# A decoder layer on one core: q and k normalised, turned and scaled beside the projection, and two groups of scores ahead of a turn

## What is computed

```python
qkv = jnp.clip(jnp.einsum('bsd,ed->bse', hidden_states, Wqkv), -8.0, 8.0)
q, k, v = jnp.split(qkv, [D_MODEL, 2 * D_MODEL], axis=-1)
q = _layer_norm(q, q_ln_w, q_ln_b)
k = _layer_norm(k, k_ln_w, k_ln_b)
# 32 heads of 32
scores = jnp.einsum('bqhd,bkhd->bhqk', q, k) * scale + slopes * rel   # causal
out = jnp.einsum('bhqk,bkhd->bqhd', softmax(scores), v).reshape(B, S, D_MODEL)
...
x = x + _L0_attn_ref(_layernorm(x), ...)
x = x + _L0_xattn_ref(_layernorm(x), ctx_4096, ctx_4096, ...)   # softmax of q over the head, of k over the positions
x = x + _L0_ffn_ref(_layernorm(x), ...)
```

## Time and profile before

| What | Value |
|---|---|
| Median of 3 runs | 3303.28 us (3303.07 to 3303.88) |
| Span of the profiled execution | 3299.9 us |
| What lies around the span, median less span | 3.4 us |
| TensorE busy | 3128.8 us, 95% |
| Weight loads busy | 2393.9 us, 73% |
| VectorE busy | 1773.3 us, 54% |
| ScalarE busy | 1045.8 us, 32% |
| GpSimd busy | 507.1 us, 15% |
| Mean granted TensorE clock | 0.977 of full |
| Moved by the transfers | 66 GB/s on average |

### The profile page before, as it was taken

The page is one execution under the profiler, slowest core; times in us unless marked ns, Lnnn a source line. Parts: engine busy times, 40 slices in busy tenths (PEclk is TensorE's granted clock), DMA queues, the critical chain, the costliest instruction groups (busy, mean ns, idle before and its releaser), DMA issues. The chain is left out here.

```text
span 3299.9 us, 41826 instructions
## 1 busy us (share of the span) xinstructions
PE 3128.8 (95%) x15136; PEld 2393.9 (73%) x15136; DVE 1773.3 (54%) x2927; ACT 1045.8 (32%) x2356; POOL 507.1 (15%) x525
## 2 busy tenths in 40 slices
PE   7999997799999999999996799999999899999998
PEld 6888886566666666666663688888887788888887
DVE  5311112466666666666663655555555655555555
ACT  2100000566665566666651211111111211111111
POOL 2100000233333333333332100000000100000000
PEclk9999999899999999999996899999999999999999
DMA  4222223111111111111110432222122521231222
GB/s 144 93 73 75 73 70 116 41 39 38 43 46 51 38 38 39 50 38 51 38 33 31 129 82 55 76 65 75 54 82 76 153 64 54 81 81 54 62 74 78
DMA packets 83350, 218.73 MB, mean 66 GB/s; under 512 B 11984, under 2 KB 18256, under 8 KB 81232
## 3 DMA queue, kind: packets, MB, share of 16 engines
q1 hardware_dynamic: 83280, 217.78, 21.8%
HBM read 175.79 MB, written 41.94 MB: 66 GB/s over the span
## 5 line engine op out<-in xcount | busy, mean ns | idle before, releaser
L312 PE MATMUL ff_ps<-h_xT_hi,w_hi 128*128 128x512 f32 x1376 | 538.2, 391 | 13.2 <-DVE h_xT_lo L96 13.2
L312 PE MATMUL ff_ps<-h_xT_lo,w_hi 128*128 128x512 f32 x1376 | 537.1, 390 | 0.0
L312 PE MATMUL ff_ps<-h_xT_hi,w_lo 128*128 128x512 f32 x1376 | 537.0, 390 | 0.0
L1042 ACT ACTIVATE w_hi<-words 128x1024 fp32r<-128x1024 f32 x134 | 142.5, 1063 | 697.3 <-DVE words L1087 697.3
L1127 DVE TENSOR_TENSOR acc<-ff_po,acc 128x512 f32<-128x512 f32 x352 | 243.0, 692 | 210.6 <-PE ff_po L312 209.9
L312 PE MATMUL qkv_acc<-w_hi,xT_hi 128*128 128x512 f32 x768 | 300.9, 392 | 9.2 <-DVE w_lo L255 9.2
L312 PEld LDWEIGHTS ff_ps<-h_xT_hi,w_hi 128*128 128x128 f32 x1376 | 259.5, 189 | 68.3 <-issue 8.8
L312 PE MATMUL qkv_acc<-w_hi,xT_lo 128*128 128x512 f32 x768 | 299.4, 390 | 0.0
L312 PE MATMUL qkv_acc<-w_lo,xT_hi 128*128 128x512 f32 x768 | 299.3, 390 | 0.0
L312 PEld LDWEIGHTS ff_ps<-h_xT_hi,w_lo 128*128 128x128 f32 x1376 | 259.4, 189 | 54.1
L312 PEld LDWEIGHTS ff_ps<-h_xT_lo,w_hi 128*128 128x128 f32 x1376 | 259.6, 189 | 53.8
(11 more groups left out here) (156 smaller groups left out, 5305.9 us busy)
## 6 DMA issues: line engine op xcount, KB each, us to landing
words<-in_w SPq DMA_DIRECT2D x90, 512.0 KB, 3.5
qkv<-qkv_out SPq DMA_DIRECT2D x96, 256.0 KB, 2.0
words<-in_w SPq DMA_DIRECT2D x176, 128.0 KB, 4.0
sc<-in_s SPq DMA_DIRECT2D x88, 256.0 KB, 4.3
qk_in<-qkv SPq DMA_DIRECT2D x16, 1024.0 KB, 4.9
w_stage<-in_w_attn SPq DMA_DIRECT2D x56, 256.0 KB, 3.0
qkv_rows<-in_x SPq DMA_DIRECT2D x16, 512.0 KB, 3.8
ctx_in<-in_context SPq DMA_DIRECT2D x16, 512.0 KB, 3.7
```

The lines of the kernel that those rows point to most:

```text
L312: last = nc.tensor.matmul(out, left, right, start=n == 0, stop=n == len(pairs) - 1)
L1042: nc.scalar.activation(dst, src, ACT.Copy).then_inc(s["split_hi"], 1)
```

## The change

**The projection** now works in two halves of eight tiles. Each half goes through all six chunks, so there are twelve rounds of eight tiles, and the weights are read twice. A round loads the eight pieces of the next one, one with every tile. The first chunk is loaded at once into the room of `head_left`, in four loads. Behind the second chunk of q, and of k, a tile's 1024 columns lie whole in SBUF (`head_left`, `head_right`). VectorE adds their statistics, GpSimd normalises (`normalise_heads`), TensorE turns them one tile later (`turn_heads`), ScalarE scales them (`scale_heads`), and SyncE stores them into `qh` and `kh` two tiles later. In round 5 the x tiles of the second half are loaded, normalised, turned and split.

**The attention** loads q as it is and k straight into the blocks of `kD` (`load_heads`). `transpose_qk`, `norm_qk_affine`, `qk_statistics`, `normalise_qk` and `key_blocks` go. A turn's first two groups of scores, its first tile of keys with the exponentials and transposes, the transposes of group 0's probabilities and the context's transposes are now done in the tail of the turn ahead of it (`second_lead`, `lead_scalar`), or, for turn 0, ahead of the loop. The twelve steps follow with everything two steps earlier (j for t - 2). The reciprocal norms are spread by eight transposes of a column that is read 128 times, in place of the diagonal matrix. The memset of `kD` stands first in the attention's setup, and SyncE waits for it. Outside these phases only unused semaphores and a size of scratch memory for transfers change.

The core of the diff:

```diff
+    TILES = NB // 2
+    ROUNDS = 2 * QKV_CHUNKS
+    xT_hi = sb("xT_hi", [P, TILES, KT, P], F32R, ph)
+    xT_lo = sb("xT_lo", [P, TILES, KT, P], F32R, ph)
...
+            def load(ci, r):
+                sp.wait_ge(s["w_lo_done"], ci * KT + r - 1)
+                chunk = ci % QKV_CHUNKS if ci < ROUNDS else QKV_CHUNKS
+                sp.dma_start(stage[:, r % 2, :], w_attn[chunk, :, r, :]).then_inc(w_in[r % 2], 16)
+
+            def load_rows(n):
+                if n >= 2:
+                    sp.wait_ge(ln.transposed, n + 1)
+                sp.dma_start(rows[:, n % 2, :], x[n, :, :]).then_inc(x_in[n % 2], 16)
+
+            def store_heads(m):
+                half, kind, t = m // (2 * TILES), m // TILES % 2, m % TILES
+                sp.wait_ge(s["h_out"], m + 1)
+                sp.dma_start((qh, kh)[kind][half * TILES + t, :, :],
+                             flat(heads[:, m % 2, :, :])).then_inc(h_stored[m % 2], 16)
...
+            for ci in range(ROUNDS):
+                half, chunk = half_and_chunk(ci)
+                for t in range(TILES):
+                    load(ci + 1, t)
+                    if ci == 0 and t + 3 < TILES:
                         load_rows(t + 3)
-                    if t % 2 == 0:
-                        load(c + 1, t // 2)
-                    sp.wait_ge(clipped, c * NB + t + 1 + BANKS)
-                    sp.dma_start(qkv[t, :, bass.ds(c * N, N)], res[:, :]).then_inc(stored, 16)
-
-            chunks(sp, chunk)
-            sp.wait_ge(stored, 16 * (QKV_CHUNKS * NB + 1))
+                    if ci == 4 and t < 2:
+                        load_rows(TILES + t)
+                    if (m := follows(ci, t, 2)) is not None:
+                        store_heads(m)
+                    if chunk >= 4:
+                        n = values_before(ci, t)
+                        sp.wait_ge(s["clipped"], ci * TILES + t + 1)
+                        sp.dma_start(v[half * TILES + t, :, (chunk - 4) * N:(chunk - 3) * N],
+                                     res[:, n % 2, :]).then_inc(v_stored[n % 2], 16)
+                    if ci == 5 and t + 2 < TILES:
+                        load_rows(TILES + t + 2)
...
+            def normalise_heads(m):
+                t, p = m % TILES, m % 2
+                pool.wait_ge(s["h_mom"], m + 1)
+                nc.gpsimd.tensor_tensor(h_mom[:, p, 4:5], h_mom[:, p, 3:4], half_neg[:, :], ALU.pow).then_inc(
+                    s["h_rstd"], 1)
+                pool.wait_ge(s["h_rstd"], m + 1)
+                for part in (left[:, t, :], right[:, p, :]):
+                    last = nc.gpsimd.tensor_scalar(part, part, h_mom[:, p, 2:3], h_mom[:, p, 4:5], ALU.add, ALU.mult)
+                last.then_inc(s["h_normed"], 1)
...
+            def scale_heads(m):
+                kind = m // TILES % 2
+                if m == 0:
+                    act.wait_ge(s["affine_in"], 4 * 16)
+                act.wait_ge(s["h_turned"], m + 1)
+                if m >= 2:
+                    act.wait_ge(h_stored[m % 2], m // 2 * 16)
+                for k in range(KT):
+                    last = nc.scalar.activation(heads[:, m % 2, k, :], room[m % 2][:, k, :], ACT.Identity,
+                                                scale=affine[:, 2 * kind, k:k + 1],
+                                                bias=affine[:, 2 * kind + 1, k:k + 1])
+                last.then_inc(s["h_out"], 1)
...
+                if chunk < 4:
+                    dve.wait_ge(s["clipped"], at + 1)
+                    first = chunk % 2 * 6
+                    nc.vector.bn_stats(h_stats[:, t, first:first + 6], dst).then_inc(s["h_stats"], 1)
...
+            def part(ci, t):
+                hi, lo, at = w_hi[ci % 2], w_lo[ci % 2], ci * TILES + t
+                for k in range(KT):
+                    if ci == 0 and t == 0:
+                        pe.wait_ge(s["w_lo_done"], k + 1)
+                    for n, (a, w) in enumerate(((xT_hi, hi), (xT_hi, lo), (xT_lo, hi))):
+                        last = nc.tensor.matmul(acc[:, at % 4, :], a[:, t, k, :], w[:, k, :],
+                                                start=k == 0 and n == 0, stop=k == KT - 1 and n == 2)
+                last.then_inc(s["mm_done"], 1)
...
+            def turn_heads(m):
+                pe.wait_ge(s["h_normed"], m + 1)
+                if m >= 2:
+                    pe.wait_ge(s["h_out"], m - 1)
+                for k in range(KT):
+                    part_of = (left[:, m % TILES, :], right[:, m % 2, :])[k // 4]
+                    last = nc.tensor.transpose(room[m % 2][:, k, :], part_of[:, k % 4 * P:(k % 4 + 1) * P], ident[:, :])
+                last.then_inc(s["h_turned"], 1)
...
+                    part(ci, t)
+                    if (m := follows(ci, t, 1)) is not None:
+                        turn_heads(m)
+                    if ci == 5:
+                        if t == 0:
+                            pe.wait_ge(s["h_out"], 2 * TILES)
+                        ln.transpose(pe, TILES + t, t % 2, room[t % 2])
...
+    def load_heads(sp, b):
+        sp.dma_start(hT[:, :, :], qh[b, :, :].rearrange("p (a d) -> p a d", a=KT)).then_inc(s["q_loaded"], 16)
+        for j in range(HG):
+            at = slice(j * HD, (j + 1) * HD)
+            sp.dma_start(kD[at, :, j, :], kh[b, at, :].rearrange("p (a d) -> p a d", a=KT)).then_inc(s["kd_loaded"], 16)
+
+    def scores(pe, b, t):
+        nc.tensor.matmul(bank_s[:, :], hT[:, t, :], flat(kD[:, t, :, :]), start=True, stop=True).then_inc(
+            s["s_done"], 1)
...
         if ahead:
-            pe.wait_ge(s["p_out"], (b + 1) * G)
+            pe.wait_ge(s["q_loaded"], (b + 2) * 16)
+            pe.wait_ge(s["kd_loaded"], (b + 2) * HG * 16)
             if cross:
                 pe.wait_ge(s["y_out"], b)
             else:
-                pe.wait_ge(s["s_biased"], (b + 1) * G)
-            transpose_qk(pe, b + 1)
+                pe.wait_ge(s["m_out"], (b + 1) * XT)
+            scores(pe, b + 1, 0)
...
+            keys(pe, b + 1, 0)
         if cross:
-            if ahead:
-                pe.wait_ge(s["a_out"], 2 * b + 4)
-            pe.wait_ge(s["n_diag"], c + 1)
-            for e, bank in enumerate(norm_banks):
-                last = nc.tensor.matmul(bank, ones[:, :], flat(diag[:, 4 * e:4 * e + 4, :]), start=True, stop=True)
+            pe.wait_ge(s["n_pow"], c + 1)
+            pe.wait_ge(s["y_out"], c + 1)
+            for k in range(KT):
+                last = nc.tensor.transpose(norm_banks[k // 4][:, k % 4, :],
+                                           n_sq[:, 1, k:k + 1].to_broadcast([P, P]), ident[:, :])
             last.then_inc(s["r_done"], 1)
+        if ahead:
+            second_lead(pe, b + 1)
...
+    def second_lead(pe, b):
+        pe.wait_ge(s["s_biased"], b * G + 1)
+        scores(pe, b, 1)
+        turn_probabilities(pe, b, 0)
+        turn_keys(pe, b, 0)
+        pe.wait_ge(s["kt_out"], b * XT + 1)
+        transpose_context(pe, b)
...
         if ahead:
-            norm_qk_affine(act, b + 1)
-            context_out(act, b + 1)
+            lead_scalar(act, b + 1)
+
+    def lead_scalar(act, b):
+        exponentials(act, b, 0)
+        key_exponentials(act, b, 0)
+        exponentials(act, b, 1)
+        probabilities_out(act, b, 0)
+        keys_out(act, b, 0)
+        context_out(act, b)
...
+            key_maxima(dve, b + 1, 0)
...
+            bias_scores(dve, b + 1, 1)
+            maxima(dve, b + 1, 1)
+            reciprocals(dve, b + 1, 1)
```

More of the change, by code:

```diff
@@ L235, in _ @@
+            for r in range(KT // 2):
                 high(0, r, w_hi[0])
-            ln.high(act, 0, 0, turn[0])
-            for r in range(PIECES // 2, PIECES):
+            ln.high(act, 0, 0, room[0])
+            for r in range(KT // 2, KT):
                 high(0, r, w_hi[0])
-            def chunk(c, parity, first):
-                if not first:
-                    act.wait_ge(mm_done, c * NB)
-                for t in range(NB):
-                    if first and t + 1 < NB:
-                        ln.high(act, t + 1, t + 1, turn[(t + 1) % 2])
-                    if t % 2 == 0:
-                        high(c + 1, t // 2, w_hi[1 - parity])
@@ L249, in _ @@
-            chunks(act, chunk)
+            for ci in range(ROUNDS):
+                if ci:
+                    act.wait_ge(s["mm_done"], ci * TILES)
+                for t in range(TILES):
+                    if ci == 0 and t + 1 < TILES:
+                        ln.high(act, t + 1, t + 1, room[(t + 1) % 2])
+                    high(ci + 1, t, w_hi[1 - ci % 2])
+                    if (m := follows(ci, t, 1)) is not None:
+                        scale_heads(m)
+                    if ci == 5:
+                        ln.high(act, TILES + t, t, room[t % 2])
@@ L265, in _ @@
             statistics(1)
-            for r in range(1, PIECES // 2):
+            for r in range(1, KT // 2):
                 low(0, r, w_hi[0], w_lo[0])
-            ln.low(dve, 0, 0, turn[0])
```

(39 more changed lines are left out.)

592 lines of the change are left out of this document (288 added, 304 removed).

## The result

The changed kernel takes 3328.61 us (median of 4 runs: 3326.89, 3327.0, 3330.23 and 3357.04), before 3303.18. The slowest of the four had a granted clock of 0.917 where the others had 0.97; with it the ratio of the means is 1.0097 (95% interval 1.0078 to 1.0116), without it 1.0075 and the median 3327.0. The kernel is slower by 25.4 us, by 23.8 without that run; forecast were 3321 and slower.

The account below looks back on a forecast made before the run. TensorE, close to full in all three stages, was taken as the bound. Terms -9.5 + 29.1 + 6.6 + 0.5 - 4.5 - 5.0 + 3.8 - 3.2 = +17.8 on 3303.3 gave 3321 us; range 3296 to 3343, its own 3310 to 3332.

Parts of the forecast that it names:

- Prologue: Start of the projection: first weights land in four loads, so products start at 14.6, not 24.07; -9.5 us.
- Head transposes: Projection: 32 head tiles at 0.91 us each on TensorE, with no wait ahead of them; +29.1 us.
- contention that I kept as a rival: Projection: GpSimd and VectorE contend, so a head tile's chain outgrows its 6.35; +5 us, 3326, double at most; chance 0.07.
- Half boundary: Round 5 into round 6: VectorE falls behind on x tiles, the eighth weight piece is late; 5.1 plus 1.5 clock, +6.6 us.
- Weight supply: Value rounds of the projection: load loop of 5.4 against 5.44 just holds, last piece 0.25 late at two rounds' starts; +0.5 us.
- products in the value rounds wait: Sign in the projection's value rounds by which the prediction called itself wrong; no size given.
- rival 4: Value rounds: weight pieces land in 3.8, not 3.0, so the loop is 6.2; +22 us, 3343; chance 0.10.
- Transition: Projection's end to turn 0: 45.0 becomes 40.5, output weights landing 23.6 behind the products; -4.5 us, bounds -7 and 0.
- Tails: Turns 1 to 14: waits of 0.65 and 3.3, -9.8 us, and clock falls in every turn, +13.6; together +3.8.
- tail of turn 0: End of attention turn 0: 25.17 becomes 18.7 with waits of 1.4 and 2.5, plus 1.5 for the clock; -5.0 us.
- Last turn: End of the attention: diagonal product goes, two matmuls of 1.9 each become eight transposes of some 2.0 in all; -3.2 us.
- rival that the lead hides its waits: Attention tails: all 3.95 per turn and the clock falls go, decided at ScalarE's exponentials of group 1; 3240; chance 0.08.

Follow-up runs that it names:

- doubled run: On the changed kernel, the eight transposes of a head tile in the projection run twice over, same result: 3355.8 us, 27.2 more.
- run with the weights first: On the changed kernel, SyncE issues the output weights' four loads ahead of q and key blocks, and they are split ahead of other setup: 3324.36 us, 4.2 less.
- run with the keys first: On the changed kernel, ScalarE copies the turned keys out ahead of the exponentials of group 1: 3275.4 us, 53.2 less.
- filled run: On the changed kernel, three more passes of the tail's eight key transposes, same place and values, run where TensorE would stand: 3309.8 us, 18.8 less.

## Why the prediction was right, point by point

**Prologue, right.** 24.07 to 14.78 is 9.3; forecast 9.5.

**Head transposes, right, both the price and that nothing hides them.** 32 x 0.91 fill the stage's sum below, and the doubled run adds 0.86 for each tile. The contention that I kept as a rival didn't come: the six rows of `w_lo` that take 0.80 to 1.43 all lie in round 0, beside GpSimd's normalising of x as in the earlier trace rows. In the head rounds VectorE's subtraction never runs beside GpSimd's halves. At 4 of the 32 head tiles it ends ahead of them, at the other 28 it starts 0.15 to 0.22 behind their end, held until then by ScalarE's `w_hi`:

```profile
72.89 0.68 DVE L321 TENSOR_TENSOR w_lo<-w_stage,w_hi 128x512 fp32r<-128x512 f32 x1
...
80.90 0.69 DVE L321 TENSOR_TENSOR w_lo<-w_stage,w_hi 128x512 fp32r<-128x512 f32 x1 [2.48 <-ACT w_hi L284]
```
```profile
74.08 0.77 POOL L263 TENSOR_SCALAR head_left<-head_left,head_mom 128x512 f32<-128x512 f32 x1
...
79.91 0.77 POOL L263 TENSOR_SCALAR head_right<-head_right,head_mom 128x512 f32<-128x512 f32 x1
```

What the Trainium skill says of shared SBUF interfaces (GPSIMD Engine Reference, section Specifications) fits the rows of 1.43. In the head rounds the two miss each other by 0.2; the prediction had no reason for that, so this part of it is luck.

**Half boundary, the mechanism right, the sum right by luck.** Ahead of the first product of round 6 and in it 4.1 + 2.5 = 6.6 were lost (a tile step of 10.46 in place of 6.36, then 7.91 in place of 5.44), as forecast. VectorE does fall behind as I had it, by 0.7 to 1.1 a tile. It starts the statistics of the last x tiles 7.12 and 7.44 apart (the last of these three rows is at 301.92), where TensorE's tile takes 6.35:

```profile
287.36 0.69 DVE L63 BATCH_NORM_STATS2 ln_stats<-qkv_rows 128x6 f32<-128x512 f32 x1 [3.12 <-DMA qkv_rows<-in_x]
...
294.48 0.69 DVE L63 BATCH_NORM_STATS2 ln_stats<-qkv_rows 128x6 f32<-128x512 f32 x1 [3.01 <-DMA qkv_rows<-in_x]
```

But TensorE had more room than I gave it: it waits 0.70 and 2.97, where I had 0.7, 1.1 and 3.3, so 3.7 for 5.1. The fall of the clock behind them, 2.5 of it in the first product of round 6, makes most of the other 2.9, for which I had 1.5. Two misses of opposite sign make the 6.6.

**Weight supply, mis-sized.** Forecast +0.5, measured 1.2 and 1.3 at the starts of rounds 5 and 11. The median landing of all pieces is 3.3, not 3.0; in round 4 ScalarE starts on most pieces 3.1 to 3.3 behind their issue, on the first 3.8. So the loop takes 5.6 against 5.44, and the eighth piece is late. By its own words the prediction was wrong "if products in the value rounds wait": they do, twice for 1.0, far from the 22 of rival 4. -9.3 + 29.1 + 6.6 + 2.5 = +28.9, against a measured +29.0.

**Transition, the term that failed.** Forecast -4.5, measured -0.3. I had all four loads of the output weights landed 23.6 behind the products. The first was split at 24.5, the last at 28.3, since they land 1.25 apart behind the loads of q, of the key blocks and of the rest. VectorE's lead starts behind the last subtraction, at 620.0, 30.5 behind, where I had 25.9. The run with the weights first shows that cause.

**Tails, the waits right within 0.2, the turn and the clock mis-sized.** 0.65 and 3.3 were forecast, 0.49 and 3.25 came, and by the released engine and its order: the run with the keys first takes 2.14 off. What was off is the fall's price. I took 1.51 a turn from the kernel before. It was 1.6 in every second turn and 2.6 in the others. In all of them the context's transposes took 1.97 for 1.09 and the next scores 1.74 to 1.92 for 1.02; in the longer ones the queries (835.41, 1.91 for 1.02) and the keys behind them were slow as well. A turn at the upper clock throughout would be about 71.3, an estimate: the 71.80 of the filled run less the 0.5 by which its transposes delay the copy. That is 1.05 less a turn than before (-14.7; forecast -9.8), and leaves +29.3 for the falls, less 7.6 of before (+21.7; forecast +13.6). The two make the measured +7.0 by the way they are found; what the runs show is that both were too small, with opposite signs. That +3.8 came near +7.0 is in part luck.

In the tail of turn 0 the waits were 1.37 and 2.06 (forecast 1.4 and 2.5), and a fall cost 2.8 (forecast 1.5): 0.9 of the sum.

**Last turn, the term right, the clock left out.** -3.2 forecast, -6.6 measured. Two stretches, one of each kernel, from the end of `project(1)` of the last own turn to the feed-forward:

```profile
1776.80:1841.04 64.24, 30.73 (x97) 14.87 (x95) 23.66 (x48) 12.61 (x20) 19.76 (x19) 0.76 0.13 48
```
```profile
1745.41:1816.10 70.69, 39.13 (x90) 17.51 (x88) 25.55 (x49) 12.62 (x20) 19.79 (x19) 0.64 0.12 43
```

The norms at the end save 3.1, as forecast. The transposes start 4.0 behind the column sums (1821.07 and 1825.02), where the matmuls did so 5.2 behind them (1793.02 and 1798.21); the feed-forward starts 16.0 behind the norms, not 17.9.

```profile
1825.02 1.12 PE L754 MATMUL bank_q<-ident,n_sq 128*128 128x128 f32 x4 [2.00 <-POOL n_sq L837]
```

The norms of the last own turn, at the start of the stretch, save nothing (0.1), since the queries behind them wait for GpSimd. The rest is the clock: it came back to its upper level amid the queries, which take 28.9 to the first use of their output where they took 32.7.

The forecast of 3321 was 7.6 low: 4.2 of it the transition, 2.3 the projection, 3.2 the turns, 0.9 the tail of turn 0, 0.3 the feed-forward, less 3.4 of the last turn, where the forecast had no term for the clock. The sign, the two large terms (head transposes, tails) and their mechanisms hold; sizes were missed in both directions, and that they cancel in part is luck. The rival that the lead hides its waits was false for this order of ScalarE, and true one line further on: its place was named rightly, ScalarE's exponentials of group 1.

## What to carry to other kernels

When work is moved ahead on one engine, write out the order of every engine that follows it: here two scores, a key tile and their exponentials were put ahead of the turn, and 53 us hung on whether ScalarE copies the keys, for which TensorE waits, ahead of exponentials for which nobody waits yet. Price a pause on TensorE twice, by its length and by the clock behind it. A load that stands behind a store on one queue has a loop of its own; compare its period with the tile's by the measured landing, and see that 0.1 or 0.2 over in each tile is paid at the end of the round.

## What was not expected of the hardware

The granted clock isn't a matter of the pause's length alone. A pause of 3.25 behind one of 0.49 let it fall in 14 of 14 tails (in each of four kernels), 1.11 behind 0.49 in none (two kernels), 2.11 in 5 of 14 in the kernel before and in 2 of 14 in the same kernel with 0.84 less work in its turn. In the kernel before the five falls stand in every third turn. And a fall has two costs: losses of 1.6 and 2.6 us took turns, so turns of 72.9 and 73.9 alternate. No run here shows what sets this rhythm. The last turn kept the lower level in some kernels (clock 0.64) and regained the upper in others, 5 us apart, without an edit in it.
